# A windowed-attention layer stack on one core: the next layer's first two units moved into the feed-forward tail of the layer ahead

## What is computed

```
x = x + 0.5 * FFN(layernorm(x))
x = x + GlobalAttention(layernorm(x))
x = x + 0.5 * FFN(layernorm(x))        # the same weights as the first
```

```
for i in range(6):
    x = attn_layer(shift_tokens(x), Wqkv[i], q_scale[i], k_scale[i], Wo[i]) + x
    x = ffn_layer(shift_tokens(x), ln_g[i], ln_b[i], W1[i], b1[i], W2[i], b2[i]) + x
```

## Time and profile before

| what | value |
|---|---|
| median of 3 runs | 4699.27 us (4692.64 to 4707.0) |
| the profiled execution | 4695.61 us, its span 4693.8 us |
| busy shares | PE 86%, PEld 66%, DVE 80%, ACT 65%, POOL 43% |
| mean granted clock of PE | 0.953 |
| DMA | 88.78 MB, mean 19 GB/s |

### The profile page before, as it was taken

The page is one execution under the profiler, slowest core; times in us unless marked ns, Lnnn a source line. Parts: engine busy times, 40 slices in busy tenths (PEclk is TensorE's granted clock), DMA queues, the critical chain, the costliest instruction groups (busy, mean ns, idle before and its releaser), DMA issues. The chain is left out here.

```text
span 4693.8 us, 116229 instructions
## 1 busy us (share of the span) xinstructions
PE 4058.7 (86%) x42352; PEld 3115.0 (66%) x42352; DVE 3754.1 (80%) x7533; ACT 3051.5 (65%) x4888; POOL 2034.4 (43%) x1420
## 2 busy tenths in 40 slices
PE   5988988989989889938858689899899898898898
PEld 4866857857758768616535478578577587686685
DVE  7988979979979889845335389799799798798897
ACT  5866857848848758612413478488488487586685
POOL 5544536535536545320010155265355365354452
PEclk9999999999999999967968899999999999999999
DMA  1000000000000000040030000000000000000000
GB/s 51 9 24 14 8 31 7 9 29 9 23 14 9 22 17 8 6 95 2 1 81 2 25 17 9 30 8 8 28 9 23 14 9 22 15 9 24 13 8 13
DMA packets 30619, 88.78 MB, mean 19 GB/s; under 512 B 7504, under 2 KB 13648, under 8 KB 28368
## 3 DMA queue, kind: packets, MB, share of 16 engines
q1 hardware_dynamic: 29104, 80.95, 6.4%
q10 hardware_dynamic: 1152, 3.15, 0.3%
HBM read 38.72 MB, written 1.05 MB: 8 GB/s over the span
## 5 line engine op out<-in xcount | busy, mean ns | idle before, releaser
L780 POOL TENSOR_TENSOR pool<-pool 128x512 f32<-128x512 f32 x768 | 1177.1, 1563 | 1147.0 <-DVE pool L878 1147.0
L450 PE MATMUL psum<-squares,pool 128*128 128x128 f32 x3072 | 710.0, 278 | 66.3 <-POOL pool L784 35.6
L452 PE MATMUL psum<-squares,pool 128*128 128x128 f32 x3072 | 700.2, 275 | 0.0
L492 PE MATMUL psum<-wqkv_hi,xs_lo 128*128 128x512 f32 x1152 | 514.0, 446 | 110.4 <-DVE pool L878 45.5
L867 DVE TENSOR_REDUCE pool<-pool 128x16 f32<-128x1024 f32 x384 | 453.4, 1216 | 177.9 <-ACT pool L694 174.6
L483 PE MATMUL psum<-pool 128*64 128x128 f32 x6144 | 539.5, 289 | 61.7 <-ACT pool L670 54.7
L655 ACT COPY pool<-psum 64x512 f32<-64x512 f32 x768 | 447.3, 582 | 215.2 <-PE psum L452 209.9
L450 PEld LDWEIGHTS psum<-squares,pool 128*128 128x128 f32 x3072 | 432.7, 141 | 149.3 <-issue 61.1
L670 ACT COPY pool<-pool 32x512 f32<-32x512 f32 x768 | 486.7, 634 | 9.0
L694 ACT ACTIVATE pool<-psum 128x1024 f32<-128x1024 f32 x384 | 376.5, 1023 | 171.6 <-PE psum L494 167.7
L493 PE MATMUL psum<-wqkv_lo,xs_hi 128*128 128x512 f32 x1152 | 461.7, 401 | 0.0
(11 more groups left out here) (167 smaller groups left out, 8172.0 us busy)
## 6 DMA issues: line engine op xcount, KB each, us to landing
pool<-pool SPq DMA_DIRECT2D x192, 128.0 KB, 2.3
pool<-in_wqkv SPq DMA_DIRECT2D x12, 1536.0 KB, 6.1
k_st<-turn_st SPq DMA_DIRECT2D x8, 1536.0 KB, 21.4
pool<-in_wo SPq DMA_DIRECT2D x12, 512.0 KB, 3.5
pool<-in_w SPq DMA_DIRECT2D x12, 341.0 KB, 3.0
pool<-in_w SPq DMA_DIRECT2D x12, 192.0 KB, 2.8
rotary<-in_rotary SPq DMA_DIRECT2D x2, 1024.0 KB, 5.1
pool<-in_scale SPq DMA_DIRECT2D x12, 128.0 KB, 6.6
```

The source lines that it names most:

```text
L450: pe.matmul(o, by_cos[:, p // 2, 2 * c:2 * c + 2, :], ident, start=True, stop=False, is_transpose=True)
L452: last = pe.matmul(o, by_sin[:, p // 2, 2 * c:2 * c + 2, :], ident, start=False, stop=True, is_transpose=True)
L492: pe.matmul(o, xs_lo[:, k % 2, :], wqkv_hi[:, c], start=True, stop=False)
L780: last = g.tensor_tensor(by_sin[:, q, :, hd * r:hd * r + hd], qn[:, q, :, hd * (1 - r):hd * (2 - r)], tab, ALU.mult)
```

## The change

It has these parts.

- **Openings.** The q and k products, the squares and the norms of the next layer's unit 0 move into chunk 1 of the tail; those of unit 1 into chunk 2, with unit 0's normalising and cosine products ahead of them on DVE; the first half of unit 0's v product into chunk 3. Unit 1's q and k are normalised after `result(3)`. Step 0 of `attention` falls away, and step 1 (`if k == 1`) is what is left: turning and scores of unit 0, the second half of its v product, v of unit 1. Unit 2's `take` on ACT now stands behind unit 0's key copies.
- **Banks.** So that banks 0 to 3 are free for the openings, chunks 1 to 3 use banks 4 to 7 alone: every up product in 6 and 7 (`up_bank`), mean, variance and spread in 4 or 3, every down product in 5. An up product therefore waits for the hidden product just ahead of it (`done(C, NF, j - 1)`), where it waited for the one before that.
- **Chunk 0.** Its first up product and `mean(1)` come ahead of unit 14's values; `centre(1)` ahead of unit 15's probabilities on DVE; the squares and the first gelu ahead of `products(14)` on ACT.
- **Layer loop.** The loop body runs five times (`layers`), with the openings of the next layer in it, and the last layer is written out behind it without them. Each half's first two units are opened ahead of the loop. POOL's and SP's programs are unchanged.

```diff
-            return 3 if c else 0
+            return (0, 3, 4, 4)[c]
...
-        def down_bank(c):
-            return 5 if c + 1 < CHUNKS else 7
+        def up_bank(c, j):
+            return 6 if c else 2 * (j % 2)
+        DOWN_BANK = 5
...
+            def layers(eng, layer):
+                with eng.Fori(0, DEPTH - 1) as l:
+                    layer(l, True)
+                layer(DEPTH - 1, False)
...
+                    def three_passes(o, k, c):
+                        pe.matmul(o, xs_lo[:, k % 2, :], wqkv_hi[:, c], start=True, stop=False)
+                        pe.matmul(o, xs_hi[:, k % 2, :], wqkv_lo[:, c], start=False, stop=False)
+                        return pe.matmul(o, xs_hi[:, k % 2, :], wqkv_hi[:, c], start=False, stop=True)
+                    def qk_products(U, k):
+                        pe.wait_ge(lo_ready, done(U))
+                        for j in range(4):
+                            if j % 2 == 0:
+                                pe.wait_ge(qn_ready, done(U - 1, 2, j // 2))
+                            last = three_passes(bank(j), k, slice(512 * j, 512 * j + 512))
+                            if j % 2:
+                                last.then_inc(qk_ready, 1)
+                    def v_products(U, k, parts, alone):
+                        pe.wait_ge(lo_ready, done(U))
+                        pe.wait_ge(s_taken, done(U - 2))
+                        if alone:
+                            pe.wait_ge(v_out, done(U - 1))
+                        for j in parts:
+                            last = three_passes(bank(4 + j), k, slice(2 * INNER + 512 * j,
+                                                                      2 * INNER + 512 * j + 512))
+                        if 1 in parts:
+                            last.then_inc(v_ready, 1)
+                    def open_first(l):
+                        pe.wait_ge(w_split, done(l + L0))
+                        qk_products((l + L0) * UNITS, 0)
+                    def open_v(l):
+                        v_products((l + L0) * UNITS, 0, (0,), True)
+                    def open_second(l):
+                        qk_products((l + L0) * UNITS + 1, 1)
...
+                            if k == 1:
+                                def rest_of_v():
+                                    pe.wait_ge(x_ready, done(C0 - 1))
+                                    v_products(U0, 0, (1,), False)
+                                turned_scores(U0, 0, 0, True, middle=rest_of_v,
+                                              between=lambda: v_products(U, 1, range(2), True))
+                                return
...
-                            else:
-                                pe.wait_ge(hid_ready, done(C0 + c - 2, NF, 1))
+                            elif c > 1:
+                                pe.wait_ge(xn_ready, done(C0 + c - 1))
...
-                            pe.wait_ge(hid_ready, done(C, NF, j - 2))
-                            if j == 1 and c + 1 < CHUNKS:
+                            if c:
+                                pe.wait_ge(hid_ready, done(C, NF, j - 1))
+                            else:
+                                pe.wait_ge(hid_ready, done(C, NF, j - 2))
+                            if c == 0 and j == 1:
                                 pe.wait_ge(xc_ready, done(C + 1))
+                            if c == 1 and j == 0:
+                                pe.wait_ge(y_ready, done(U0 + UNITS - 1))
...
+                        pe.wait_ge(w_ffn, (l + L0 + 1) * 48)
+                        mean(1)
+                        up(0, 0)
                         values(W0, 3, 2)
-                        pe.wait_ge(w_ffn, (l + L0 + 1) * 48)
-                        for c in range(CHUNKS):
-                            more = c + 1 < CHUNKS
-                            if more:
-                                mean(c + 1)
-                            up(c, 0)
-                            if c < 2:
-                                output(W0, 2 + c)
-                            if more:
-                                variance(c + 1)
-                            up(c, 1)
-                            up(c, 2)
-                            down(c, (0,))
-                            if more:
-                                spread(c + 1)
-                            down(c, range(1, NF - 1))
-                            if c == 0:
-                                values(W0, 3, 3)
-                            down(c, (NF - 1,))
+                        variance(1)
+                        up(0, 1)
+                        output(W0, 2)
+                        up(0, 2)
+                        spread(1)
+                        down(0, (0, 1))
+                        values(W0, 3, 3)
+                        down(0, (2,))
+                        output(W0, 3)
+                        up(1, 0)
+                        if more_layers:
+                            pe.wait_ge(hid_ready, done(C0, NF, NF - 1))
+                            open_first(l + 1)
+                        up(1, 1)
+                        mean(2)
+                        down(1, (0,))
+                        up(1, 2)
+                        variance(2)
+                        down(1, (1,))
+                        spread(2)
+                        down(1, (2,))
+                        up(2, 0)
+                        mean(3)
+                        if more_layers:
+                            open_second(l + 1)
+                        up(2, 1)
+                        down(2, (0,))
+                        variance(3)
+                        up(2, 2)
+                        down(2, (1,))
+                        spread(3)
+                        down(2, (2,))
+                        up(3, 0)
+                        if more_layers:
+                            pe.wait_ge(xn_ready, done(C0 + 3))
+                            open_v(l + 1)
+                        up(3, 1)
+                        down(3, (0,))
+                        up(3, 2)
+                        down(3, (1, 2))
+                    open_first(0)
+                    open_v(0)
+                    open_second(0)
+                    layers(pe, layer)
...
+                            if k == 1:
+                                turned(U0, 0, (0, 1))
+                                keep_v(U0, 0, 0)
+                                turned(U0, 0, (2, 3))
+                                take(l, 0, 2)
+                                keep_v(U, 0, 1)
+                                return
...
+                        a.wait_ge(w_ffn, (l + L0 + 1) * 48)
+                        squares_of(1)
+                        gelu(0, 0)
+                        gelu(0, 1)
+                        diagonal(last)
+                        gelu(0, 2)
+                        products(last)
+                        if more_layers:
+                            take(l + 1, 0, 0)
+                        gelu(1, 0)
+                        if more_layers:
+                            square_qk(N0)
+                        squares_of(2)
+                        gelu(1, 1)
+                        gelu(1, 2)
+                        if more_layers:
+                            take(l + 1, 0, 1)
+                        gelu(2, 0)
+                        squares_of(3)
+                        if more_layers:
+                            square_qk(N0 + 1)
+                        gelu(2, 1)
+                        gelu(2, 2)
+                        for j in range(NF):
+                            gelu(3, j)
+                    take(0, 0, 0)
+                    square_qk(L0 * UNITS)
+                    take(0, 0, 1)
+                    square_qk(L0 * UNITS + 1)
+                    layers(a, layer)
...
+                    def open_norms(l, n):
+                        norms((l + L0) * UNITS + n)
+                    def open_first(l):
+                        normalise_qk((l + L0) * UNITS)
+                        v.wait_ge(turn_ready, done(l + L0))
+                        cosine((l + L0) * UNITS, 0)
...
+                            if k == 1:
+                                cosine(U, 0)
+                                less_top(U - 1)
+                                return
...
+                        centre(1)
                         for piece in probabilities(W0 + 3):
                             piece()
-                        for c in range(CHUNKS):
-                            more = c + 1 < CHUNKS
-                            if more:
-                                centre(c + 1)
-                            hidden(c, 0)
-                            if c < 2:
-                                residual(W0 + 2 + c, 3, 2 + c)
-                            if more:
-                                deviation(c + 1)
-                            for j in range(1, NF):
-                                hidden(c, j)
-                            if more:
-                                normal(c + 1)
```

(40 more changed lines are left out.)

185 lines of the change are left out of this document (78 added, 107 removed).

## The result

The changed kernel takes 4946.77 us (median of 4 runs, 4937.91 to 4960.06) where the kernel before took 4703.14 beside it (4 runs, 4692.64 to 4708.66): a ratio of 1.0521, 95% interval 1.0501 to 1.054. It is slower, as forecast, but by 244 us and not by 157: the time lies above the range of 4785 to 4895.

What follows compares the result with a forecast made beforehand. Bound taken: each layer boundary's PE-ACT-DVE chain, then 27.4 us in which the next layer starts from nothing. 8 x 13.5 + 2 x 9.7 + 2 x 14.0 + 2 = +157 us on 4695.6, median 3.7 above: 4857 us; range 4785 to 4895.

Steps and rivals of the forecast that it cites:

- what the change does not touch: Units 2 to 14 of each layer, with their interleaved steps, keep their pace: no term in the sum.
- the tails: Last layer of each half, without openings but with the same banks: +7.9 us at full clock, +14.0 with clock, twice.
- E: Last down product to the next layer's `less_top(0)`: 10.1 us without jump, 12.7 with, against 27.4; -17.3 or -14.7.
- A: Chunk 0, up product ahead of unit 14's values: chunk 1's first product starts at 662.6 against 665.25, -2.7 us.
- B: Chunk 1, with unit 0's q and k products and one pair of up banks: 20.5 us against 12.1, +8.4.
- C: Chunk 2, with unit 0's normalising and cosine products and unit 1's norms: 22.4 us against 10.2, +12.2.
- D: Chunk 3, up products no longer alternating between two pairs of banks: 11.2 us against 8.2, +3.0.
- the jump itself: Layer loop's jump back, formerly hidden under the wait for x: 2.6 us exposed (bounds 0 and 3.5), at eight boundaries.
- the clock: Half-clock spells on PE after four gaps per boundary: 0 to 10.3 us, taken as 7.3, or 6.1 without jump.
- Rival 1: Clock stays full in PE's gaps: only +75 us, 4774 us; chance 0.12.
- Rival 2: Half clock through all of chunk 3, its serial chain keeping PE half busy: 72 us more, 4929 us; chance 0.10.
- Rivals 3 and 4: Chunks 1 to 3 grow less: faster, 4653 us, below 17.4 (chance 0.05); or evens out near 17.4, 4699 us (0.03).

Runs made afterwards that it cites:

- after_p: Changed kernel with 192 semaphore increments put where PE waits anyway, shifting PE's second-half code at no cost; 4878.49 us, ratio 1.0384.
- fill: Changed kernel with zero-matrix products put into PE's waits ahead of chunk 0's first up product, spread(2) and spread(3); 4866.9 us, ratio 1.0343.
- unroll: Changed kernel with all six layers of each half written out on PE, ACT and DVE instead of looped; 4880.68 us, ratio 1.0376.
- ends: Changed kernel with the next layer's openings moved out of chunks 1 to 3 to behind chunk 3, single pair of up banks kept; 4940.51 us, ratio 1.0506.
- c0: Kernel before with chunk 0's new order alone; chunks 1 to 3, banks and opening as before; 4703.44 us, ratio 1.0008.
- v1b_p: v1b with 182 semaphore increments in two PE waits, shifting the second half's inner loop; 4621.66 us, ratio 0.9834 to the kernel before.
- v1b: Changed kernel with chunks 0 to 2 as before; chunk 3 alone has one bank pair and unit 0's opening; 4683.03 us, ratio 0.9964.
- pad64: Changed kernel with 64 unused semaphore increments on PE, once, ahead of the second half's first layer; 4902.33 us, ratio 1.0412.
- bfill: Kernel before with four unread products put into PE's wait of 4.5 us ahead of variance(1); 4691.06 us, ratio 0.9987.

## Why the prediction was wrong, and where it was right

**The step that failed is one that was not there.** The prediction took for granted that "what the change does not touch (units 2 to 14, with their interleaved steps) keeps its pace". It did in half 0 (1430.7 us for 1436.4 over six layers), and not in half 1, where PE's inner jump came to cost 4 us and a spell at half clock twice a layer (+50.3 us over six layers). With the boundaries of half 1 that is 68 us, taken away by nothing but a shift of the code (after_p). Without it the changed kernel stands at 4878.5 us, 21 above my 4857 and inside the range. The order of instructions shows that PE's code grew (the layer is now written out twice per half), and the earlier trace rows had a jump of 3.51 us. I priced that one at its own place and did not ask what other jumps might cost at another. Why PE waits there is not shown; that the place decides is. The 21 us that are left are the boundaries' (149 us over ten for 127), the tails' (36 for 28), and 5 less in the layers.

**The sum per boundary** was 13.5 us; it measured 17.9, in these terms (full clock by fill's boundary, E by unroll's):

| term | predicted | measured |
|---|---|---|
| A at full clock | -2.7 | 28.54 - 30.06 = -1.5 |
| B at full clock | +8.4 | 20.8 - 12.1 = +8.7 |
| C at full clock | +12.2 | 22.4 - 10.2 = +12.2 |
| D at full clock | +3.0 | 11.9 - 8.2 = +3.7 |
| E without a jump | -17.3 | 10.1 - 27.4 = -17.3 |
| the jump itself | +2.6 | 2.8 (PE's issue wait) |
| the clock | +7.3 | 6.3 in chunks 0 to 3, and 3.1 behind the jump |

**B, C and E** are right to a few tenths. (The terms listed for E add up to 11.2 and not 10.1: in unroll ACT's first copy starts 1.0 us behind the last down product, so not all of the transposes stand on the path.) That norms and deviations stand ahead of the next up product in DVE's one queue is shown by where the openings stand: C takes 13.5 us without them (ends) and 24.4 with them (after_p).

**The clock** is right in size for the chunks (6.1 without the jump; 6.3 in this boundary, 4.5 in fill's mean) and wrong in where: I tied it to four waits of 2.6 us and more, and it fell behind one of 2.13 us too (at 672.08), and in ends behind waits of 1.6 to 2.5 us. Behind the jump I had 1.7 us at most, the transposes; there were two spells, on the transposes and on the scores, 3.1 us. The miss of 4.4 is, to a rounding, 2.1 of clock, 1.2 of A, 0.7 of D, 0.3 of B and 0.2 of the jump. The Trainium skill's TensorE: Matmul & The Clock Gate (HAM oscillation) says that a loop whose waits idle TensorE pays for the warm-up each time (it ties that to waits of a certain length, which my sentence left out). With all four spells paid I had 10.3 us, and the rows have 9.4: nearer than my 7.3, in part by luck, since the rows have six spells and not those four.

**The jump.** PE waits 2.76 us at the outer jump and, at some places, about 4 at the inner, with nothing to wait for. The Trainium skill's Runtime: NRT & Kernel Launch (Instruction fetch mechanics) says that a taken branch out of the fetched code stalls; these waits agree, though no row shows a fetch. The Trainium skill's Advanced Engine Details and Errata (Control Flow Timing) gives a compare-and-branch 0.1 us; the good places look like that from outside (after_p's products follow at once). My choice of the row over that figure was right, and too narrow.

**A**: the gain of 2.7 us is not there. The 1.5 us in the table are fill's A without a spell against an A of the kernel before that has one, so they aren't the order's alone. In the kernel before the new order makes +3.7 us in A and -1.8 in B where nothing disturbs it, and is lost in the spread of A elsewhere (c0). The working followed PE's chain alone; as I read the rows, unit 14's values, put behind the up product, also come later for ACT and DVE, which I didn't follow. That wasn't tried by itself.

**The tails** of the last layers were to cost 14 us each; the last one cost 18.4, the middle's whole stretch 13.9. Chunks 0 to 3 of the middle's tail take 28.3 + 20.3 + 12.9 + 11.7 = 73.2 us for 53.4, so 19.8; what took 6 of it back within the middle is not known.

**Rivals.** Rival 1 (the clock stays full) is refuted by the rows of 0.50. Rival 2 (half clock through chunk 3) is refuted too: from 733.0 to 741.4 the clock is 1.00, and D grew by 4.2 us. Rivals 3 and 4 are refuted by the chunks' growth: 9.7 + 13.6 + 4.2 = 27.5, where they needed 17.4 or less.

**What stays open.** Which places are bad for PE's inner loop: its jump back stalled at 4 of the 12 that unroll has, and I found no rule in where they lie. Half 1's boundaries of the kernel before are 5 us longer than half 0's: in four of the five `normal` takes 5.1 to 5.6 us beside POOL, for 2.4, and E is 29.7 to 31.1 for 27.4, with ACT's issue wait at the jump 3.0 to 3.3 us for 2.1. The kernel before was never shifted, so how much of that its place makes is open. And v1b_p with its layers unrolled wasn't tried; its boundaries without a jump (above) don't promise more.

## What to carry to other kernels

Work that is moved under a chain lengthens the chain where it stands in an engine's queue ahead of the chain's next link. Here it paid to move it under the last chunk alone and to leave the double buffers of the others: chunk 3 grew by 4.5 us and the opening fell by 11.7 (v1b_p, 1.7% faster than before, some of it perhaps by half 1's place; against after_p, 3.8% slower with three chunks serial). After any edit that changes the length of an engine's code, compare the stretches that the edit doesn't touch, and if they moved, shift the code by instructions put into a wait before judging the edit: here that was 68 us of 244 (64 by the ratios), and it hid 61 us of v1b's gain.

## What the hardware did that I had not expected

- A semaphore increment on PE took 0.15 us: 192 of them 28 us, (32.23 - 3.74) / 192, and in pad64 0.14 each, (12.42 - 3.74) / 64.
- The same inner loop jumps back on PE without a wait at one place and with 3.98 us at another, 64 instructions away (pad64), and half clock follows.
- A spell at half clock that was filled away at one wait came back at waits of the opening that had had none (bfill), so that filling gave 4.5 us a boundary (6.3 at best) where it covered three waits in a row and 0.6 where it covered one.
- A DVE operation of 0.55 us took 4.56 beside a POOL operation and ended 0.3 us after it, and so in ten layers of every version but pad64, which has nine (1.0 to 5.7 us).
